# Routed experts of a mixture layer: every expert on every token, or each expert on its own tokens in 23 tiles of 128 slots

## The chip, the cores and the metric

The kernel runs on one core of a Trainium2 chip. The metric is the device time of one execution in microseconds (us); lower is better. The engines of the core work side by side: TensorE (PE, matrix products; the loading of its stationary operand is listed as PEld), VectorE (DVE), ScalarE (ACT), GpSimd (POOL) and SyncE (SP, which here only issues DMAs). Each has its own program and waits for the others on semaphores. TensorE's clock is 2.4 GHz when granted in full (shown as 1.00) and 1.2 GHz at its lower level (0.50).

## What is computed

The reference is two transformer-like layers on x of 2 x 512 tokens by 256 features: a time-mixing block, an expert-choice mixture, a delta-rule attention, and last the mixture that this change touches. Cut to that last part (D = 256, 8 experts, the two best per token, shared width 1024, routed width 128):

```
g = x @ sw1.T
u = x @ sw2.T
shared_out = jax.nn.silu(g) * u @ sw3.T
scores = jax.nn.sigmoid(x @ router_w.T)
_, top_idx = jax.lax.top_k(scores + expert_bias, TOPK)
top_scores = jnp.take_along_axis(scores, top_idx, axis=-1)
top_scores = top_scores / (top_scores.sum(-1, keepdims=True) + 1e-09)
combine = jnp.zeros((T, E), x.dtype).at[jnp.arange(T)[:, None], flat_idx].add(flat_sc)
h12 = jnp.einsum('td,ehd->teh', flat_x, w12)
h1, h2 = jnp.split(h12, 2, axis=-1)
h = jax.nn.silu(h1) * h2
out_e = jnp.einsum('teh,edh->ted', h, w3)
routed_out = jnp.einsum('ted,te->td', out_e, combine).reshape(b, s, d)
return shared_out + routed_out
```

x going in is layer-normed, and the result is layer-normed and added to x. Each of the 1024 tokens has two experts, so of the 8 x 1024 (expert, token) products that the reference writes down, 2 x 1024 have a weight other than zero.

## The kernel before

Activations lie in SBUF as 8 tiles (`NT`) of 128 tokens by 256 features. The last stage is `expert_mixture`. It turns the normed input `xm` into features-on-partitions form, splits it and all weights into a rounded part (HI, cast by ACT) and a rest (LO, a subtraction on DVE), and writes each product as three matmuls (HI*HI, HI*LO, LO*HI): `PRODUCTS`.

The work is a row of 32 steps (`STEPS`): for each half of the tokens (512), 8 blocks of 128 shared hidden features and then 8 experts of 128 hidden features, all treated alike. In a step n:

- `up(n)` (line 2108), PE: 6 matmuls for the gate and 6 for the up part, each 512 tokens wide, into a pair of PSUM banks;
- `silu(n)` (2166), ACT, on the gate; the product with the up part (2290), DVE;
- for an expert, the product with its tokens' shares (2219), POOL, which reads `share`, a 128 x 1024 tile for each expert;
- `high(n)` (2177), ACT, and the rest by POOL (2225): the two parts of the hidden features in `hidden_r`;
- `down(n)` (2124), PE, three steps (`LAG`) behind `up`: 12 matmuls of 256 columns that add to the output of the half in PSUM banks 0 to 3.

PE's order is written by hand: `up(n)`, then `down(n-3)`. Beside this, weights are cast during the first 10 steps (2146 on ACT, 2238 on DVE), two groups of four tiles a step. The router's scores come after `up(0)` (2087); DVE takes the two best (`choose`, 2252 to 2260) after step 1 and works out the shares (`weigh`, 2262) after step 2; PE turns them (2094), and SP sends them to DRAM (`share_dram`, 2196) and back, repeated on all 128 partitions (2202). At the end DVE copies the half's output from PSUM (2279), takes the statistics of the norm (292, 296), normalizes (308), adds to x (2324), and SP writes x out (2207).

## Time and profile before

| | us |
|---|---|
| median of 3 runs | 485.63 |
| lowest and highest | 484.15, 485.74 |
| the profiled execution | 489.34 |
| its span, first to last instruction | 487.6 |
| PE busy | 368.9 (76%) |
| DVE busy | 298.2 (61%) |
| ACT busy | 248.8 (51%) |
| POOL busy | 118.0 (24%) |

A chain of waits is followed back from the last instruction: at each step to what released it. PE has 29% of the span on that chain, all of it in the last stage, which starts at about 326 us. Times below count from the start of the span. "idle before" is how long an engine stood still just before an instruction, with the work that released it.

### The profile page before, as it was taken

To read this page: it belongs to the slowest core of one execution; us is meant where nothing else is said; L and a number is where in the kernel's file an instruction comes from. 1 tells how busy PE (TensorE), PEld (TensorE's weight loads), DVE (VectorE), ACT (ScalarE), POOL (GpSimd) and SP (SyncE) were. 2 spreads that over 40 slices of the span, in tenths; PEclk is the share of its full clock that TensorE was granted. 3 is DMA by queue.
4 is the path that set the end of the run, shared out by engine and by line. 5 is a ranking of instruction groups with operands and counts; after the bars stand their busy time and mean duration, and the time that the engine had idled before them with its cause. 6 is when DMAs were issued, how large, how long until landed. Compare 5 with 4: busy or idle time off the path is not lost. (4 is left out here: it accounts for less than half of the span.)

```text
span 487.6 us, 10066 instructions
## 1 busy us (share of the span) xinstructions
PE 368.9 (76%) x4130; PEld 293.4 (60%) x4130; DVE 298.2 (61%) x633; ACT 248.8 (51%) x460; POOL 118.0 (24%) x142
## 2 busy tenths in 40 slices
PE   2999877955799775332077899818999999999990
PEld 1544566855578664221066465607888888888880
DVE  5899997777245547999952667774774211311127
ACT  2889755475366755764133457547755333322230
POOL 5493002300000105000044200000244664335640
PEclk9999989888999788555579759977899999999996
DMA  7790000000000000000000000000024300000002
GB/s 230 240 342 4 0 1 0 2 0 0 1 3 2 3 3 0 1 1 0 0 1 4 3 5 3 3 1 1 0 73 146 131 0 1 1 1 2 0 1 86
DMA packets 12489, 15.82 MB, mean 32 GB/s; under 512 B 2046, under 2 KB 10644, under 8 KB 12444
## 3 DMA queue, kind: packets, MB, share of 16 engines
q1 hardware_dynamic: 12444, 15.18, 9.7%
q8 instruction: 33, 0.54, 0.5%
q14 instruction: 12, 0.10, 0.1%
HBM read 14.09 MB, written 1.08 MB: 31 GB/s over the span
## 5 line engine op out<-in xcount | busy, mean ns | idle before, releaser
L2225 POOL TENSOR_TENSOR hidden_r<-third,hidden_r 128x512 fp32r<-128x512 f32 x31 | 41.1, 1327 | 140.4 <-ACT hidden_r L2177 140.4
L2290 DVE TENSOR_TENSOR third<-third,ps 128x512 f32<-128x512 f32 x32 | 22.0, 687 | 84.8 <-PE ps L2108 79.5
L2124 PEld LDWEIGHTS ps<-down_r,hidden_r 128*128 128x128 f32 x384 | 49.2, 188 | 3.2 <-POOL hidden_r L2225 0.9
L2124 PE MATMUL ps<-down_r,hidden_r 128*128 128x256 f32 x384 | 50.3, 281 | 0.7 <-POOL hidden_r L2225 0.7
L2177 ACT CAST hidden_r<-third 128x512 fp32r<-128x512 f32 x32 | 19.9, 623 | 59.5 <-PE ps L2124 59.5
L2108 PE MATMUL ps<-xm_r,gate_r 128*128 128x512 f32 x192 | 50.1, 397 | 0.0
L2108 PE MATMUL ps<-xm_r,up_r 128*128 128x512 f32 x192 | 49.9, 396 | 0.0
L2108 PEld LDWEIGHTS ps<-xm_r,up_r 128*128 128x128 f32 x192 | 36.9, 192 | 7.9
L1509 PE MATMUL ps<-ident,area 128*128 128x128 f32 x32 | 8.5, 416 | 40.4 <-DVE area L1835 40.4
L2108 PEld LDWEIGHTS ps<-xm_r,gate_r 128*128 128x128 f32 x192 | 34.6, 191 | 5.7 <-issue 0.2
L1509 PEld LDWEIGHTS ps<-ident,area 128*128 128x128 f32 x32 | 5.6, 212 | 43.2 <-DVE area L1835 43.2
L1832 DVE TENSOR_TENSOR third<-area 128x124 f32<-128x124 f32 (+15 forms) x31 | 29.2, 943 | 1.1
L2166 ACT ACTIVATE third<-ps 128x512 f32<-128x512 f32 x32 | 19.2, 599 | 20.7 <-PE ps L2108 20.7
L1835 DVE TENSOR_TENSOR area<-area,third 128x124 f32<-128x124 f32 (+15 forms) x31 | 27.9, 901 | 1.1
L1737 ACT COPY area<-third 32x128 f32<-32x128 f32 x64 | 18.9, 295 | 14.7 <-DVE third L1879 13.4
L1681 ACT ACTIVATE area<-ps,own_side 128x512 f32<-128x512 f32 (+1 forms) x16 | 15.9, 1100 | 20.2 <-PE ps L1509 20.2
L1130 POOL TENSOR_SCALAR keys_by_head<-k_t,own_fourth 128x512 f32<-128x512 f32 x4 | 3.9, 984 | 82.8 <-ACT k_t L1275 82.8
L1162 PE MATMUL ps<-w_r,x_r 128*128 128x512 f32 x96 | 19.2, 350 | 3.6 <-DVE beta_rows L1355 2.1
L2219 POOL TENSOR_TENSOR third<-third,stored 128x512 f32<-128x512 f32 x15 | 19.4, 1291 | 0.0
L1162 PEld LDWEIGHTS ps<-w_r,x_r 128*128 128x128 f32 x96 | 14.9, 188 | 7.0 <-issue 3.5
L1180 PE MATMUL ps<-proj_rows,third 128*32 128x128 f32 x384 | 15.5, 293 | 4.7 <-ACT qkv L1301 4.0
L1582 PE MATMUL ps<-area,k_t 128*32 128x128 f32 x128 | 16.3, 353 | 1.7 <-DVE area L1888 0.7
(340 smaller groups left out, 835.1 us busy)
## 6 DMA issues: line engine op xcount, KB each, us to landing
stored<-share_dram SPq DMA_DIRECT2D x8, 512.0 KB, 5.8
stored<-in_L_ffn_sw_dram SPq DMA_DIRECT2D x3, 1024.0 KB
stored<-in_L_ffn_w_dram SPq DMA_DIRECT2D x1, 2048.0 KB
x<-L_attn_hidden_state_dram SPq DMA_DIRECT2D x4, 256.0 KB, 3.5
out_dram<-x SPq DMA_DIRECT2D x4, 256.0 KB, 2.4
w_nat<-in_L_attn_Wk_dram SPq DMA_DIRECT2D x1, 256.0 KB, 2.7
w_nat<-in_L_attn_Wv_dram SPq DMA_DIRECT2D x1, 256.0 KB, 2.9
w_nat<-in_L_attn_Wr_dram SPq DMA_DIRECT2D x1, 256.0 KB, 4.1
```

The source lines that it names most:

```text
L1162: last = nc.tensor.matmul(ps[:, bank, 0:cols.stop - cols.start], own, w_r[:, wp, ci, cols], start=i == 0, stop=i == len(passes) - 1)
L1582: last = nc.tensor.matmul(ps[strand[q], WS_BANK, 0:P], w_t[:, n, q, :], state_before(n)[:, q], start=True, stop=True, skip_group_check=True)
L1737: nc.scalar.copy(u_place[strand[q], n % U_SLOTS, :, q, :], u[strand[q], n % U_KEPT].rearrange("p (h e) -> p h e", h=HH)) \
L1832: link(V.tensor_tensor(part, rows.unsqueeze(3).to_broadcast([P, below, G, j + 1]), inv[:, j, :, 0:j + 1].unsqueeze(1).to_broadcast([P, bel ...
L1835: last = V.tensor_tensor(inv[:, j + 1:, :, 0:j + 1], inv[:, j + 1:, :, 0:j + 1], part, ALU.subtract)
L2108: last = nc.tensor.matmul(ps[:, bank + which, :], w[:, wp, c, a, :], xm_r[:, xp, c, b * T:(b + 1) * T], start=i == 0, stop=i == C * len(PR ...
L2124: last = nc.tensor.matmul(ps[:, t // 2, t % 2 * D:(t % 2 + 1) * D], hidden_r[:, n % 2, hp, t * P:(t + 1) * P], down_r[:, wp, a, :], start= ...
L2166: a(gated[:, n % 2, :], ps[:, 4 + 2 * (n % 2), :], ACT.Silu).then_inc(silu_ready, 1)
L2177: nc.scalar.copy(hidden_r[:, n % 2, HI, :], hidden[:, n % 4, :]).then_inc(hidden_hi, 1)
L2219: nc.gpsimd.tensor_tensor(hidden[:, n % 4, :], hidden[:, n % 4, :], share[:, a - SH, b * T:(b + 1) * T], ALU.mult) \
L2225: nc.gpsimd.tensor_tensor(hidden_r[:, n % 2, LO, :], hidden[:, n % 4, :], hidden_r[:, n % 2, HI, :], ALU.subtract).then_inc(hidden_lo, 1)
L2290: V.tensor_tensor(hidden[:, n % 4, :], gated[:, n % 2, :], ps[:, 4 + 2 * (n % 2) + 1, :], ALU.mult) \
```

## The change

The routed experts leave the row of steps. The steps are now 16, shared features only (`STEPS` = B * SH). After step `EARLY` = 10 come 23 tiles (`SLOTS`) of 128 token slots; each tile belongs to one expert, whose number is only known at run time. 23 = 16 full tiles for 2048 rows and at most 7 more, since an expert's last tile may be partly filled.

- After the choice of experts, PE counts (`count`, two matmuls with a table of ones and a triangle): for each token, how many before it went to the same expert. DVE makes of that a slot number for each token's first and second expert (`place_tokens`: 12 small instructions up to `slots`, 3 more up to `owner`, the expert of each tile).
- POOL writes the rows of `xm` to those slots in DRAM by 16 indirect DMAs of 128 rows of 1 KB (`rows_dram`); SP reads them back as tiles (`rows`), 8 tiles and then 15.
- For each tile j, PE turns the rows (2 transposes), loads the owner's number into a register (`own_expert`), multiplies with weights at an address made of that register (`up_routed`, 6 matmuls of 256 columns: gate and up side by side), turns the product (1 transpose) and multiplies down (`down_routed`, 3 matmuls of 256 columns). ACT makes the rounded parts, the silu, and copies the result out (`keep_rows`); DVE makes the rests and the product.
- SP writes the results to DRAM in four parts, POOL gathers them again by 16 indirect DMAs (`found`), and DVE adds them with the shares (`combine`).
- POOL no longer computes in the stage; the rest of `hidden_r` is made by DVE. The shares are no longer turned, nor sent through DRAM.
- Early in the program three DMAs fill `rows_dram` with input rows, so that unused slots hold finite numbers, and 16 more small memsets run on POOL.

```diff
+    SLOTS = 2 * NT + E - 1
+    STEPS, EARLY, LAG = B * SH, 10, 3
+    SLOTS_FIRST = NT
+    RESULT_PARTS = ((0, 8), (8, 16), (16, 20), (20, SLOTS))
...
+                def own_expert(j):
+                    expert[j] = nc.tensor.value_load(owner[0:1, j:j + 1], min_val=0, max_val=E - 1)
...
+                def turn_rows(j):
+                    if j in (0, SLOTS_FIRST):
+                        pe.wait_ge(rows_in[j // SLOTS_FIRST], 16)
...
+                def up_routed(j):
+                    pe.wait_ge(xm_lo_kept, TURNED + j + 1)
+                    pe.wait_ge(prod_ready, tile(j - 2) if j >= 2 else shared(EARLY - 2 + j))
+                    if j == 0:
+                        pe.wait_ge(kept_dve, len(groups))
+                    for i, (c, wp, xp) in enumerate((c, *parts) for c in range(C) for parts in PRODUCTS):
+                        last = nc.tensor.matmul(ps[:, 4 + j % 2, 0:2 * P], rows_t[j % 2][:, xp, c],
+                                                routed_up[:, wp, c, bass.DynSlice(expert[j], 1), :], start=i == 0,
+                                                stop=i == C * len(PRODUCTS) - 1)
...
+                for j in range(SLOTS + 2):
+                    if j < SLOTS:
+                        turn_rows(j)
+                        own_expert(j)
+                    if j < LAG:
+                        down(EARLY - LAG + j)
+                    if 1 <= j <= SLOTS:
+                        up_routed(j - 1)
+                    if j >= 3:
+                        turn_hidden(j - 3)
+                    if j >= 4:
+                        down_routed(j - 4)
+                up(EARLY)
+                turn_hidden(SLOTS - 1)
+                down_routed(SLOTS - 2)
+                down_routed(SLOTS - 1)
+                for n in range(EARLY + 1, STEPS + LAG):
                     if n < STEPS:
                         up(n)
...
+                sp.wait_ge(rows_out, 16 * 2 * NT)
...
+                for start, stop in RESULT_PARTS:
+                    sp.wait_ge(rows_kept, stop)
+                    sp.dma_start(tiles(core.results_dram)[:, start:stop, :], rows[:, start:stop]) \
+                        .then_inc(results_out, 16)
...
+                pool.wait_ge(routed, PLACED)
+                for t in range(NT):
+                    for k in range(2):
+                        nc.gpsimd.indirect_dma_start(core.rows_dram, bass.IndirectOffsetOnAxis(slots[:, k, t:t + 1], 0),
+                                                     xm[:, t, :], None).then_inc(rows_out, 16)
+                pool.wait_ge(results_out, 16 * (1 + len(RESULT_PARTS)))
+                for t in range(NT):
+                    for k in range(2):
+                        nc.gpsimd.indirect_dma_start(found[:, k, t, :], None, core.results_dram,
+                                                     bass.IndirectOffsetOnAxis(slots[:, k, t:t + 1], 0)) \
+                            .then_inc(results_in, 16)
...
+                def keep_first():
+                    dve.wait_ge(down_done, SH)
+                    dve.wait_ge(rows_out, 16 * 2 * NT)
                     for t in range(TB):
...
+                def combine(t):
+
+                    if t < TB:
+                        link(V.scalar_tensor_tensor(y[:, t], found[:, 0, t], share[:, 0, t:t + 1], y[:, t], ALU.mult,
+                                                    ALU.add))
+                    else:
+                        link(V.tensor_scalar(y[:, t], found[:, 0, t], share[:, 0, t:t + 1], None, ALU.mult))
+                    return V.scalar_tensor_tensor(y[:, t], found[:, 1, t], share[:, 1, t:t + 1], y[:, t], ALU.mult,
+                                                  ALU.add)
...
+                dve.wait_ge(results_in, 16 * 2 * NT)
+                for t in range(NT):
+                    last = combine(t)
```

PE's program before, in the middle of the row of steps: one `up` and one `down`, and so on to the end of the stage (names after "waits" are semaphores).

```order
713 L2108 MATMUL ps<-xm_r,gate_r 128x512 [waits prod_ready,xm_lo_kept,ffn_w_kept_dve]
714 L2108 MATMUL ps<-xm_r,gate_r 128x512 x5
715 L2108 MATMUL ps<-xm_r,up_r 128x512 x6
716 L2124 MATMUL ps<-down_r,hidden_r 128x256 [waits ffn_w_kept_dve,hidden_lo]
717 L2124 MATMUL ps<-down_r,hidden_r 128x256 x11
```

```order
831 L2202 MATMUL ps<-ident,stored 128x128 [waits xm_lo_kept]
832 L2202 MATMUL ps<-ident,stored 128x128
833 L2192 TENSOR_LOAD owner
834 L2192 ISA x2
835 L2212 ISA [waits prod_ready,xm_lo_kept]
836 L2212 MATMUL ps<-routed_up,xm_r 128x256 x2
837 L2212 ISA
838 L2212 MATMUL ps<-routed_up,xm_r 128x256
...
843 L2221 MATMUL ps<-ident,stored 128x128 [waits hidden_lo,prod_ready]
844 L2228 REGISTER_ALU [waits routed_rows_kept,hidden_lo]
845 L2228 MATMUL ps<-routed_down,xm_r 128x256 x2
```

Where one step had 24 matmuls of two widths and no register, one tile has 12 matmuls and transposes with a register load and some address arithmetic between them.

POOL's program in this stage before (its first rows; the pair L2219, L2225 goes on in this way):

```order
68 L2225 TENSOR_TENSOR hidden_r<-third,hidden_r 128x512 [waits hidden_hi] x2
69 L2225 TENSOR_TENSOR hidden_r<-third,hidden_r 128x512 [waits down_done,hidden_hi] x6
70 L2219 TENSOR_TENSOR third<-third,stored 128x512 [waits prod_ready,share_in_first]
71 L2225 TENSOR_TENSOR hidden_r<-third,hidden_r 128x512 [waits down_done,hidden_hi]
72 L2219 TENSOR_TENSOR third<-third,stored 128x512 [waits prod_ready,share_in_first]
```

POOL's program in this stage after:

```order
68 L2366 MEMSET third 128x128
69 L2367 AFFINE_SELECT third<-third 128x128 [waits masks_order]
70 L2374 DMA rows_dram<-xm,slots 2944x256 [waits tokens_routed,f_in,masks_order]
71 L2374 DMA rows_dram<-xm,slots 2944x256 x15
72 L2379 DMA stored<-results_dram,slots 128x256 [waits rows_in_second]
73 L2379 DMA stored<-results_dram,slots 128x256 x15
```

47 computing instructions have gone, and 32 indirect DMAs have come, in two runs of 16, each behind one wait.

## Rows read from the trace of the kernel before

**Rows 1.** The chain of waits, in order of time: start, us, what.

```profile
351.67 1.41 PE ps L2124 x12
...
353.08 2.73 PE ps L2108 x12
```

**Rows 2.** Who waited for whom in 335 to 490 us: total, times, longest.

```profile
POOL hidden_r L2225 <- ACT hidden_r L2177: 140.4, 31, 74.7
DVE third L2290 <- PE ps L2108: 79.5, 27, 3.5
```

**Rows 3.** Stretches: length, busy by engine, granted clock, DMA share, GB/s.

```profile
352.00:378.00 26.00, 26.00 (x156) 22.70 (x155) 16.10 (x31) 13.49 (x24) 10.16 (x7) 1.00 0.33 104
...
433.00:470.00 37.00, 37.00 (x217) 32.75 (x217) 6.69 (x10) 10.83 (x18) 20.25 (x16) 1.00 0.00 1
```

**Rows 4.** Timeline of PE: start, us, engine, line, operation, count, idle before.

```profile
72.03 2.78 PE L129 MATMUL ps<-ident,stored 128*128 128x128 f32 x24
...
255.95 0.75 PE L1543 MATMUL ps<-area,n_t 64*32 64x64 f32 x52 [1.11 <-issue]
...
341.63 2.16 PE L2108 MATMUL ps<-xm_r,gate_r 128*128 128x512 f32 x6
343.58 2.63 PE L2108 MATMUL ps<-xm_r,up_r 128*128 128x512 f32 x6
...
377.35 1.57 PE L2124 MATMUL ps<-down_r,hidden_r 128*128 128x256 f32 x12
```

**Rows 5.** Stretches with transposes alone on PE: columns as in Rows 3.

```profile
72.03:74.81 2.78, 2.78 (x25) 2.54 (x23) 2.68 (x10) 2.15 (x5) 0.00 (x0) 1.00 0.02 6
...
245.10:250.40 5.30, 5.30 (x27) 5.30 (x26) 2.83 (x7) 2.09 (x2) 0.00 (x0) 0.50 0.00 0
```

**Rows 6.** Timeline of DVE around the choice of experts.

```profile
346.32 0.69 DVE L2290 TENSOR_TENSOR third<-third,ps 128x512 f32<-128x512 f32 x1 [2.45 <-PE ps L2108]
...
350.91 0.16 DVE L2259 FIND_INDEX8 where<-best,select 128x8 uint32<-128x8 f32 x1
...
353.53 0.23 DVE L2267 TENSOR_TENSOR first<-first,second 128x64 f32<-128x64 f32 x1
353.79 0.23 DVE L2268 TENSOR_TENSOR first<-first,scores 128x64 f32<-128x64 f32 x1
```

**Rows 7.** Timeline of POOL: the same instruction twice.

```profile
359.02 2.57 POOL L2225 TENSOR_TENSOR hidden_r<-third,hidden_r 128x512 fp32r<-128x512 f32 x1 [3.85 <-ACT hidden_r L2177]
363.15 1.29 POOL L2225 TENSOR_TENSOR hidden_r<-third,hidden_r 128x512 fp32r<-128x512 f32 x1 [1.57 <-ACT hidden_r L2177]
```

**Rows 8.** Timeline of SP's queue: issuing one DMA.

```profile
7.98 0.47 SPq L166 DMA_DIRECT2D third<-in_L_ffn_expert_b_dram  x1
```

**Rows 9.** DMA issues: KB each, median us from issue to landing.

```profile
out_dram<-x SPq DMA_DIRECT2D x4, 256.0 KB, 2.4
```

**Rows 10.** A stretch of DMA traffic: POOL busy, granted clock, DMA share, GB/s.

```profile
360.00:370.00 10.00, 4.17 (x3) 1.00 0.63 215
```

**Rows 11.** Groups by form: count, busy us, mean ns, idle before.

```profile
L1719 ACT COPY k_t<-ps 128x256 f32<-128x256 f32 x4 | 1.5, 378 | 0.0
...
L907 ACT ACTIVATE raised<-logits 128x128 f32<-128x128 f32 x1 | 0.3, 309 | 2.9 <-DVE logits L949 2.9
...
L1019 DVE TENSOR_TENSOR x<-x,xf 128x256 f32<-128x256 f32 x8 | 3.3, 410 | 0.6 <-ACT xf L272 0.6
L998 DVE SCALAR_TENSOR_TENSOR over<-left,least 128x256 f32<-128x256 f32 x1 | 0.5, 483 | 0.0
```

**Rows 12.** Timeline of the end of the kernel.

```profile
475.27 1.42 DVE L2279 COPY xm<-ps 128x256 f32<-128x256 f32 x4 [2.43 <-PE ps L2124]
476.73 1.41 DVE L292 BATCH_NORM_STATS2 ln_stats<-xm 128x6 f32<-128x256 f32 x4
```

398 lines of the change are left out of this document (267 added, 131 removed).

## The prediction

> **What bounds the kernel now.** I read the chain of waits first. In the last stage it is PE alone: `down`, 1.41 us, then `up`, 2.73 us, in turn to the end [rows 1]. The stretches agree: PE is busy all of the time from 352 to 378 and from 433 to 470 us, at the full 2.4 GHz, while DVE is busy 16.1 of 26 us, later 6.7 of 37 [rows 3]. The list of waits says the same from the other side: POOL waited 140.4 us for ACT, DVE 79.5 us for PE [rows 2]. So here time is what PE has to do, 32 steps of 4.14 us = 132.5 us, and the tail behind it. A cut in PE's work counts in full, until something else is late. What the change puts beside PE are transfers and register loads of which this trace has none; they decide.
>
> **What PE loses and gains.** A `down` matmul of 256 columns takes 1.41 / 12 = 0.118 us [rows 1], a transpose 2.78 / 24 = 0.116 us at the full clock [rows 4]. 16 steps go: -66.2 us. 23 tiles come, each with 9 matmuls of 256 columns and 3 transposes: 1.06 + 0.35 = 1.41 us, together +32.4 us. If nothing else changed, 34 us would be won. The rest of the working is what of this is given back, as a line of times on the profiled execution.
>
> **Where the slots are known.** The product of step 1 starts at 346.3 us [rows 6]. Behind it now stand one rest (0.6) and one weight group (0.6) instead of two groups, then the choice. In the trace that starts at 348.96 and its last instruction ends at 351.1 [rows 6]: 2.1 us. Then three small instructions, 0.8 us. PE's `count` can so start at about 351.5, when `up(3)` is done; it takes some 0.5 us. DVE comes to `place_tokens` after the product and the rest of step 3, and that rest waits for `down(0)`: about 355.5 us. There are 12 instructions in a chain up to `slots`; the like of them stand 0.26 us apart (353.53 to 353.79) [rows 6], so 3.3 us with the longer scan: POOL gets its slots at 358.8 us. PE doesn't wait for this; DVE gets fuller in steps 4 to 9 (product, rest, up to three groups, and `weigh`: about 3.5 of PE's 4.14 us a step), close, but below PE.
>
> **The scatter.** 16 indirect DMAs on POOL, one after the other. The trace has no DMA issued by POOL. Below, SP's 0.47 us for an issue [rows 8]; above, POOL's 1.29 us for a full-width instruction, and 2.57 us for the same one when DVE works on two tiles in SBUF at the same time [rows 7]. I take 1.0 us, nearer to POOL's row, since POOL makes 128 addresses by software, though with less data than 128 x 512. 16 x 1.0 = 16.0, so 374.8; 2.4 us to land, as a store of 256 KB [rows 9]: 377.2. Then SP reads 1 MB back: 4.9 us at the 215 GB/s of [rows 10], and 1.5 us for the way: the first tile can be turned at 383.6 us. PE, with `down(6)`, is ready at about 378.4 (it ends at 378.9 in the trace [rows 4], with the turning of shares in front of it, which goes). PE stands still for 5.2 us. The three `down`s left over would fill 4.2 us of it, but `turn_rows(0)` stands ahead of them. After the pause the clock may be low: the twelve matmuls from 341.63 took 4.4 us where 2.73 is usual [rows 4]. I add 1.5 us.
>
> The Trainium skill (GPSIMD Engine Reference, section Key points) says that GpSimd shares its SBUF interfaces with VectorE and contends with DVE instructions that have two SBUF inputs. The doubled row agrees, 2.57 for 1.29 us. The scatter runs just when DVE is full of such subtractions, the gather when it is less so.
>
> **The 23 tiles.** PE needs 1.41 us a tile. ACT has two copies of 256 columns and two instructions of 128, 2 x 0.378 + 2 x 0.309 = 1.37 us; DVE 0.41 and two shorter ones, about 1.0 us [rows 11]. So ACT is just behind PE. Unknown is the register: one load, two checks and six small pieces of address work a tile in PE's sequencer. Below: nothing, if the sequencer runs ahead and PE has matmuls queued, 1.41 us. Above: the longest pause of PE for which the profile names no releaser, 1.11 us [rows 4], each time: 2.52 us. I take 1.8, since there is some queue, but the load stands right behind only two transposes. 23 x 1.8 = 41.4 us. Beside them are three `down`s (4.2 us), the wait of `down(8)` for DVE's four copies in `keep_first` (1.2 us, 1.42 less a transpose pair; it is 1.42 in [rows 12]), and at the end `up(10)` and the last tile's passage through ACT and DVE (2.7 + 1.7 us). The last result is in SBUF at 383.6 + 1.5 + 41.4 + 4.2 + 1.2 + 4.4 = 436.3 us.
>
> The Trainium skill (DMA: Bandwidth & Descriptors, section Latency and other measured facts) gives a floor of about 600 ns for a `tensor_load`. Laid on PE bare, the tile would be 2.0 us and the sum 4.8 us longer; no run here shows it yet.
>
> **The way back.** The last part of the results, 3 tiles, goes out in 3.4 us, 16 gathers take 16.0 at the same price, 2.4 to land: 458.1 us. PE meanwhile has 5 `up`s and 6 `down`s, 22.1 us, and about 1 us more since `high(n)` waits for `down(n-2)`: 459.4 us. The two are level; but behind the gather stands work on DVE that was not there. `combine` is 16 instructions of 0.41 to 0.48 us [rows 11], 7.2 us, then four tiles' statistics, 1.4 us, which stood beside PE before: 466.7. Then four additions, 1.6 us: 468.3 us. From there on it is as before from 476.73 to 487.6 [rows 12]: 10.9 us. Sum: 479.2 us against 487.6, so -8.4 us. The profiled execution has 1.7 us around its span and is 3.7 us above the median; I take the difference over to the median: 485.63 - 8.4 = 477.2 us.
>
> The terms that can move are in one line: span = 405.8 + 32 x (POOL's price of an indirect DMA) + 23 x (price of a tile), as long as POOL is later than PE at both ends. With 1.0 and 1.8 that is 479.2.
>
> **Costed at nothing.** The 16 memsets stand in front of a wait of POOL for a DMA, early in the kernel. The three filling DMAs run after the last weight load, where the transfers are idle. The rests that DVE takes over from POOL are 0.69 us and have over 3 us of DVE's waiting in each late step [rows 2]. If that cover went, each would cost 0.6 us.
>
> **Rivals.** *Both unknowns are cheap.* POOL at 0.47, tile at 1.41: the rows are there before PE is (375.1 < 378.4), the last result at 378.4 + 32.4 + 4.2 + 1.2 + 4.4 = 420.6, PE ends at 443.7, and the span is 456.1: 454 us. For it: SP issues as fast as that. Against it: POOL is the slow one wherever both do the same work.
>
> *The register load stalls PE each time.* Tile at 2.5 us: 16 us more, 495 us of span, 493. For it: the load is an instruction of the sequencer and what follows needs it. Against it: PE runs queued work while its sequencer is busy, and turning, `down` and `up` of other tiles lie between the load and its use.
>
> *POOL is slow: the case on the other side.* Its place is the two runs of 16, its price 32 times the excess. With the tile at 1.8 it eats the gain from 1.26 us on, just about the 1.29 of an ordinary full-width instruction [rows 7]; at 2.0 us the span is 511, 509 us. For it: the doubled row. Against it: a DMA of 128 rows asks less of POOL than 512 columns on 128 partitions.
>
> *The clock.* Transposes alone ran 2.78 us at 1.00, but 5.3 us at 0.50 after a pause [rows 5]. If PE stays at 1.2 GHz through the tiles, one costs 2 x 1.41 = 2.8 us: 23 us more, 500 us. The Trainium skill (TensorE: Matmul & The Clock Gate, section Part 4: PE-mode transpose) says that transposes do not engage the full clock. Against this rival: three of four instructions here are matmuls, and wide ones.
>
> **How the numbers follow.** Forecast and its neighbourhood (POOL 0.8 to 1.3, tile 1.5 to 2.2): 0.45; both cheap: 0.15; the load stalls: 0.17; POOL slow: 0.15; clock: 0.08. A measurement of this kernel can tell about 0.3% (1.5 us) from no change. Faster is the second case, 0.38 of the first and 0.03 of the third: 0.56; same 0.06; slower 0.38. The range leaves out the lower part of the cheap case and the upper part of the slow ones: 458 to 502. Faster and slower both have weight; the forecast's own range is 467 to 490 us.
>
> **What would show it.** Right: 16 POOL issues about 1.0 us apart from 359 us; PE still from 378 to 384 us; tiles 1.8 us apart; the gather landing within 2 us of PE's last `down`; 21 us from there to the end, with DVE's 16 additions ahead of the old tail. Wrong: issues over 1.26 us apart, tiles over 2.2 us apart, or a clock of 0.50 between 390 and 430 us. Wrong the other way: tiles at 1.4 us and no pause of PE before the first.

## The result, and the profile after

The changed kernel takes 495.03 us (median of 4 executions, 493.87 to 495.45) beside 485.69 us for the kernel before in the same session. The ratio is 1.020, 95% interval 1.017 to 1.023: 2.0% slower. The forecast was 477.2 us, 1.7% faster. Its range (458 to 502) holds the result, its sign was wrong. Executions of one kernel can lie 2% apart (the kernel before took 484.15 to 495.25 us here), and the profiled executions of gather_late, changed_again and all_three_paused below are such longer ones, so the experiments compare stages rather than whole executions.

The page of the changed kernel, busy time of each engine, and the stretches of its last stage (length, then busy us of PE, PEld, DVE, ACT and POOL, granted clock, DMA share, GB/s):

```profile
PE 345.4 (70%) x4018; PEld 271.0 (55%) x4018; DVE 325.6 (66%) x735; ACT 253.9 (51%) x520; POOL 91.0 (18%) x146
```

```profile
345.00:380.00 35.00, 30.14 (x173) 25.98 (x171) 23.95 (x79) 14.53 (x27) 17.22 (x16) 1.00 0.17 61
380.00:392.00 12.00, 4.59 (x21) 3.87 (x22) 7.08 (x14) 3.65 (x8) 0.00 (x0) 0.72 0.76 251
392.00:420.00 28.00, 25.96 (x184) 23.20 (x184) 12.28 (x40) 13.84 (x51) 0.00 (x0) 0.94 0.11 39
420.00:440.00 20.00, 17.83 (x120) 14.98 (x118) 8.32 (x29) 10.88 (x39) 0.00 (x0) 1.00 0.23 80
440.00:470.00 30.00, 22.24 (x107) 18.40 (x108) 6.09 (x11) 6.19 (x12) 15.18 (x16) 0.90 0.27 84
```

PE's work did shrink: 345.4 us instead of 368.9. But between 380 and 392 us, where PE was busy without a gap before (below), it is now busy for 4.6 us of 12, and it is slow again after 458 us.

```profile
380.00:392.00 12.00, 12.00 (x72) 10.65 (x71) 2.06 (x3) 3.61 (x6) 7.32 (x6) 1.00 0.16 63
```

What stands ahead of the last stage is the same code in both kernels but for the filling DMAs and the memsets, yet its length varies: the first `up` starts at 334.9 us in the profile of before and at 332.0 in that of after, and between 330 and 341 us in the profiles of the experiments. So below I compare profiled executions by the **last stage**, from the start of `up(0)` to the end: 487.6 - 334.9 = 152.7 us before, 493.1 - 332.0 = 161.1 us after, 8.4 us more. The prediction's line of times gives 479.2 - 334.9 = 144.3 us. The 16.8 us between forecast and measurement lie here (us from the start of `up(0)`, or lengths):

| piece | predicted | measured |
|---|---|---|
| slots known, scatter starts | 23.9 | 24.1 |
| from there to the first tile's turning | 24.8 | 28.6 |
| from there to the last result in SBUF | 52.7 | 56.8 |
| from there to the last gathered row | 21.8 | 24.1 |
| from there to the end | 21.1 | 27.6 |

Timelines of POOL: the first scatter issues, the last, then the first gather issues. Start, duration, and in brackets how long POOL stood idle before:

```profile
356.05 1.20 POOL L2374 DMA_INDIRECT rows_dram<-xm,slots  x1 [32.01 <-DVE owner L2446]
357.56 1.43 POOL L2374 DMA_INDIRECT rows_dram<-xm,slots  x1 [0.30 <-issue]
...
367.83 0.96 POOL L2374 DMA_INDIRECT rows_dram<-xm,slots  x1 [0.30 <-issue]
...
376.88 0.96 POOL L2374 DMA_INDIRECT rows_dram<-xm,slots  x1 [0.30 <-issue]
```

```profile
444.20 0.98 POOL L2379 DMA_INDIRECT stored<-results_dram,slots  x1 [66.36 <-DMA results_dram<-stored]
445.48 0.96 POOL L2379 DMA_INDIRECT stored<-results_dram,slots  x1 [0.30 <-issue]
```

An indirect DMA of 128 rows keeps POOL busy for 0.95 us and 0.30 us pass to the next: 1.25 us each. In the scatter four of the first five take 1.20 to 1.48 us. The scatter lasts 356.05 to 377.84, 21.8 us, the gather 19.75 us, where 16.0 each was predicted. Below them PE, the start of the tiles:

```profile
384.62 0.69 PE L2202 MATMUL ps<-ident,stored 128*128 128x128 f32 x2 [7.12 <-DMA stored<-rows_dram]
385.60 2.90 PE L2182 MATMUL ps<-down_r,hidden_r 128*128 128x256 f32 x12 [0.29 <-issue]
388.30 0.61 PE L2202 MATMUL ps<-ident,stored 128*128 128x128 f32 x2
```

`down(7)` takes 2.90 us after the pause, twice the 1.41 of [rows 1]. Then the tiles, the first matmul group of two in a row:

```profile
411.41 0.97 PE L2212 MATMUL ps<-routed_up,xm_r 128*128 x6 [0.18 <-DVE stored L2479]
...
413.16 0.98 PE L2212 MATMUL ps<-routed_up,xm_r 128*128 x6
```

Seventeen steps from 400.68 to 432.38 give 1.865 us a tile. The last surprise is behind them. PE by its own records, then ACT's `high(n)`, which waits for `down(n-2)`:

```profile
453.95 1.58 PE L2182 MATMUL ps<-down_r,hidden_r 128*128 128x256 f32 x12
455.37 1.55 PE L2166 MATMUL ps<-xm_r,gate_r 128*128 128x512 f32 x6
...
462.57 0.38 PE L2182 MATMUL ps<-down_r,hidden_r 128*128 128x256 f32 x1 [1.03 <-issue]
463.98 0.57 PE L2182 MATMUL ps<-down_r,hidden_r 128*128 128x256 f32 x1 [1.03 <-issue]
```

```profile
452.73 0.62 ACT L2294 CAST hidden_r<-third 128x512 fp32r<-128x512 f32 x1 [6.22 <-PE ps L2182]
...
466.90 0.62 ACT L2294 CAST hidden_r<-third 128x512 fp32r<-128x512 f32 x1 [13.05 <-remote]
```

By its matmul records `down(11)` (the twelve from 453.95 us) is over at 455.5, but the `high(13)` that waits for it starts at 466.90. PE itself then issues single matmuls 1.4 us apart, waiting for nothing that the profile shows. The trace also has marks of the moments at which semaphores were raised. Some are missing, in the scatter above all (the ups' semaphore has 52 marks for 55 steps); from the gather's start on those of PE's ups (each up has two) and downs are complete:

```
ups    443.2 444.5 445.9 447.2 448.6 450.0 456.2 461.1 466.9 467.0
downs  452.7 466.8 467.1 471.2 473.8 475.4
```

Up to 450.0 they come as the work is done. Then hardly one comes in 5 us, and at 466.8 to 467.1 four come in a burst: `down(11)`, both of `up(15)`, `down(12)`. The last packet of the gather is at 465.3 us, its last landing mark at 465.5. I call these PE's **held signals**. Between the first and the last of the four lie 4.2 us of matmuls (an `up` and a `down`), so the work of `down(11)` was done at least 4 us before its mark, and 11 us before by PE's own records: it is the signal that is late.

### The profile page after: what moved, and what is told of

It is laid out like the page before. It is cut to its first block and busy times, and to the rows that moved or that the text cites. A ratio compares the mean times of both kernels' runs of the same rounds, so it can differ in the third digit from the quotient of the medians.

```text
span 493.1 us, 10184 instructions
## 1 busy us (share of the span) xinstructions
PE 345.4 (70%) x4018; PEld 271.0 (55%) x4018; DVE 325.6 (66%) x735; ACT 253.9 (51%) x520; POOL 91.0 (18%) x146
## 5 line engine op out<-in xcount | busy, mean ns | idle before, releaser
L2182 PE MATMUL ps<-down_r,hidden_r 128*128 128x256 f32 x192 | 31.8, 320 | 9.6 <-issue 5.9
L2182 PEld LDWEIGHTS ps<-down_r,hidden_r 128*128 128x128 f32 x192 | 29.4, 225 | 12.3 <-issue 9.7
L2294 ACT CAST hidden_r<-third 128x512 fp32r<-128x512 f32 x16 | 9.9, 620 | 38.1 <-remote 18.6
L1520 PEld LDWEIGHTS ps<-ident,area 128*128 128x128 f32 x32 | 5.1, 194 | 43.4 <-DVE area L1846 43.4
L2379 POOL DMA_INDIRECT stored<-results_dram,slots x16 | 15.2, 949 | 70.9 <-DMA results_dram<-stored 66.4
L2166 PE MATMUL ps<-xm_r,gate_r 128*128 128x512 f32 x96 | 26.1, 408 | 2.6 <-DVE up_r L2393 2.1
L2212 PE MATMUL ps<-routed_up,xm_r 128*128 x138 | 22.8, 302 | 3.6 <-DVE stored L2479 2.9
L2166 PE MATMUL ps<-xm_r,up_r 128*128 128x512 f32 x96 | 24.4, 389 | 0.0
L2374 POOL DMA_INDIRECT rows_dram<-xm,slots x16 | 17.2, 1076 | 36.6 <-DVE owner L2446 32.0
L2212 PEld LDWEIGHTS ps<-routed_up,xm_r 128*128 128x128 f32 x138 | 18.5, 195 | 8.0 <-issue 8.0
L2166 PEld LDWEIGHTS ps<-xm_r,gate_r 128*128 128x128 f32 x96 | 17.9, 197 | 6.5 <-DVE up_r L2393 2.3
L2462 DVE TENSOR_TENSOR third<-third,ps 128x512 f32<-128x512 f32 x16 | 10.9, 683 | 15.5 <-PE ps L2139 6.0
L2166 PEld LDWEIGHTS ps<-xm_r,up_r 128*128 128x128 f32 x96 | 18.0, 188 | 3.8
```

Source lines behind the costliest of these rows:

```text
L2166: last = nc.tensor.matmul(ps[:, bank + which, :], w[:, wp, c, a, :], xm_r[:, xp, c, b * T:(b + 1) * T], start=i == 0, stop=i == C * len(PR ...
L2182: last = nc.tensor.matmul(ps[:, t // 2, t % 2 * D:(t % 2 + 1) * D], hidden_r[:, n % 2, hp, t * P:(t + 1) * P], down_r[:, wp, a, :], start= ...
L2212: last = nc.tensor.matmul(ps[:, 4 + j % 2, 0:2 * P], rows_t[j % 2][:, xp, c], routed_up[:, wp, c, bass.DynSlice(expert[j], 1), :], start=i ...
L2294: nc.scalar.copy(hidden_r[:, n % 2, HI, :], hidden[:, n % 4, :]).then_inc(hidden_hi, 1)
L2374: nc.gpsimd.indirect_dma_start(core.rows_dram, bass.IndirectOffsetOnAxis(slots[:, k, t:t + 1], 0), xm[:, t, :], None).then_inc(rows_out, 16)
L2379: nc.gpsimd.indirect_dma_start(found[:, k, t, :], None, core.results_dram, bass.IndirectOffsetOnAxis(slots[:, k, t:t + 1], 0)) \
```

## The experiments

Each ran beside the kernel before on the same chip. Ratios are to it. "First tile" is the first routed matmul, "gather" the start of the gather or of what stands in its place, both from `up(0)`; "to end" runs from the gather to the end.

| kernel | median us | ratio [95%] | last stage | first tile | gather | to end |
|---|---|---|---|---|---|---|
| changed | 495.03 | 1.020 [1.017, 1.023] | 161.1 | 61.4 | 112.2 | 48.9 |
| gather_late | 512.39 | 1.053 [1.046, 1.061] | 177.0 | 63.0 | 134.8 | 42.2 |
| pe_padded | 496.32 | 1.022 [1.012, 1.031] | 158.5 | 59.8 | 109.7 | 48.8 |
| downs_first | 499.11 | 1.028 [1.016, 1.039] | 159.6 | 61.3 | 110.7 | 48.9 |
| fixed_weights | 487.86 | 1.005 [1.001, 1.009] | 152.0 | 60.8 | 103.2 | 48.8 |
| plain_gather_pool | 486.72 | 0.999 [0.994, 1.004] | 154.2 | 63.5 | 114.9 | 39.3 |
| plain_gather_sp | 486.83 | 0.997 [0.992, 1.002] | 150.6 | 61.3 | 111.0 | 39.6 |
| registers_spread | 489.96 | 1.007 [1.003, 1.011] | 156.7 | 65.9 | 107.8 | 48.9 |
| half_rows | 476.62 | 0.980 [0.974, 0.986] | 142.5 | 53.3 | 103.2 | 39.3 |
| gather_later | 499.03 | 1.027 [1.019, 1.034] | 163.8 | 62.2 | 119.2 | 44.6 |
| changed_again | 497.49 | 1.018 [1.011, 1.025] | 162.8 | 62.5 | 114.0 | 48.8 |
| two_pauses | 493.68 | 1.014 [1.008, 1.019] | 157.1 | 61.9 | 113.3 | 43.8 |
| tail_early | 489.89 | 1.008 [1.004, 1.012] | 155.4 | 62.2 | 112.4 | 43.0 |
| all_three_spread | 485.12 | (two groups, below) | 142.6 | 58.7 | 99.2 | 43.3 |
| all_three_paused | 485.23 | 0.987 [0.983, 0.992], its five lower executions of 12 | 154.0 | 69.6 | 110.4 | 43.6 |
| all_three_again | 481.72 | 0.988 [0.983, 0.992] | 143.1 | 59.1 | 99.8 | 43.3 |
| all_four | 472.98 | 0.972 [0.967, 0.978] | 139.6 | 59.2 | 99.7 | 39.9 |

The last four columns come from one profiled execution of each kernel.

### Does PE crawl by itself, or beside the gather?

```diff
+                pool.wait_ge(down_done, shared(STEPS - 1))
                 for t in range(NT):
                     for k in range(2):
                         nc.gpsimd.indirect_dma_start(found[:, k, t, :], None, core.results_dram,
```

> One wait is added to the changed kernel: GpSimd starts its 16 gathers only after PE's last down. Nothing of the computation is left out. In the changed kernel PE crawls from 458.7 to 467 us, one matmul each 1.4 us, while the gather runs (444 to 466 us). Theory A, the gather's transfers hold up PE's supply of instructions: without a gather beside it PE runs down(11) and the rest at 0.118 us a matmul and ends its last down at about 467 us; the gather then takes 16 x 1.25 + 2.4 = 22.4 us, the tail 20: span about 509.5 us, time 511.5. Theory B, PE crawls at this place of its program whatever runs beside: last down at 475.4, span about 517.8, time 520.

Last stage 177.0 us. PE's timeline after the tiles, without a gather beside it:

```profile
465.88 1.55 PE L2166 MATMUL ps<-xm_r,gate_r 128*128 128x512 f32 x6
467.26 1.52 PE L2166 MATMUL ps<-xm_r,up_r 128*128 128x512 f32 x6
468.62 4.72 PE L2182 MATMUL ps<-down_r,hidden_r 128*128 128x256 f32 x36
```

`down(12)` to `down(14)`, which took from 458.1 to 473.8 us in the changed kernel, run through in 4.7 us. Theory A: 161.1 plus the expected 16.4 (a span of 509.5 less 493.1) is 177.5. The crawl needs the gather.

### The pause before the tiles, and the place in PE's program

```diff
+                pe.wait_ge(routed, OWNED)
+                for i in range(48):
+                    nc.tensor.matmul(ps[:, 2, 0:D], down_r[:, HI, 0, 0:P], down_r[:, HI, 1, :], start=True, stop=True)
                 for j in range(SLOTS + 2):
```

> The changed kernel with 48 more matmuls of 256 columns, whose results nobody reads, between down(6) and turn_rows(0): 48 x 0.118 = 5.7 of PE's 7.1 us idle time before the first tile. Theory A, the pause costs clock: with the pause filled, down(7) to down(9) take 1.41 us each instead of 2.90, 2.23 and 1.9, so the tiles begin about 2.8 us earlier. Rival: the wait for keep_first and for ACT and DVE takes it back, under 1 us. On the crawl of PE during the gather: if it belongs to a fetch of PE's instructions, it moves with the program, 96 instructions (some 5 to 6 us of ups and downs) earlier, to about 450 us, or falls apart; if it belongs to the gather alone, it stays at 14 us after the gather's start. Time 492 if A holds and the crawl stays as long, 484 if the crawl goes.

```profile
386.32 1.63 PE L2182 MATMUL ps<-down_r,hidden_r 128*128 128x256 f32 x12 [0.59 <-issue]
...
390.86 1.62 PE L2182 MATMUL ps<-down_r,hidden_r 128*128 128x256 f32 x12 [2.69 <-DVE xm L2494]
```

With the pause filled, the granted clock stays at 2.4 GHz (1.00 from 380 to 392 us, where the changed kernel had 0.72), `down(7)` to `down(9)` take 1.6 to 1.7 us, and the gather starts 2.5 us earlier: the clock's part of the late start, as expected. The run times do not show it: 1.022 beside 1.020, where 492 us was expected. The crawl was to move if it belonged to a fetch of PE's instructions, and did not:

```profile
460.50 0.37 PE L2182 MATMUL ps<-down_r,hidden_r 128*128 128x256 f32 x1 [1.03 <-issue]
```

It begins 15 us after the gather's start as before (14.5). The trace's queue of instruction packets (q8, 16 KB at a time) agrees: one is sent 11.7 us after the gather's start in the changed kernel and 2.7 us after it here, with the crawl at the same distance in both.

### The downs first

```diff
+                for j in range(LAG):
+                    down(EARLY - LAG + j)
                 for j in range(SLOTS + 2):
                     if j < SLOTS:
                         turn_rows(j)
                         own_expert(j)
-                    if j < LAG:
-                        down(EARLY - LAG + j)
```

> The changed kernel with down(7), down(8) and down(9) of PE ahead of turn_rows(0), and what belongs to them on ACT (the copy of hidden rows) and DVE (the rest, keep_first) ahead of the first tile's copies. All of the computation is there. Theory A: the pause of 7.1 us before the first tile takes up the downs and the wait for keep_first, 2.90 + 2.50 + 2.23 + 1.9 = 9.5 us go from behind the read, of which perhaps 1.5 come back as slow clock in the first tiles: last result about 8 us earlier, 433 us, and with the crawl of PE unchanged in length a time of about 487 us. Rival: keep_first waits for the scatter to land (379.5 us) and down(8), down(9) follow at half clock up to 388 us, behind the read: a gain of 4 us or less.

```profile
380.40 2.35 PE L2182 MATMUL ps<-down_r,hidden_r 128*128 128x256 f32 x12 [3.62 <-DVE hidden_r L2466]
386.03 5.46 PE L2182 MATMUL ps<-down_r,hidden_r 128*128 128x256 f32 x24 [3.29 <-DVE xm L2490]
```

1.5 us gained in the last stage, not 8: the rival. In the run times there is no gain: the four executions took 492.8 to 505.2 us, and 487 was expected. `down(7)` waited 3.6 us for a rest of DVE, which stood behind ACT's `high(7)` at 379.0: the signal of `down(5)`, recorded as over at 372.6, came at 378.9. So PE's signals are held at the end of the scatter too; in the changed kernel that of `down(5)` came at 379.6, which cost it little, since the rows landed at 384.6. Then `keep_first`, which must wait for the scatter, and two downs near half the clock: 2.73 us each, with 0.54 granted from 384 to 392 us.

### What the register costs

```diff
-                    expert[j] = nc.tensor.value_load(owner[0:1, j:j + 1], min_val=0, max_val=E - 1)
+                    expert[j] = j % E
```

> The changed kernel without the register: each tile takes the weights of expert j mod 8 at a fixed address, so routed results are of other experts than the tokens chose; all else is there. Theory A, the register's load and the address work set the tile's price: without them a tile goes from 1.87 us to what PE and ACT need, 1.41 to 1.45 us, 23 x 0.43 = 10 us less, time about 485 us. Rival, the tile is set by the chain of semaphores from PE over ACT and DVE and back: it stays at 1.8 to 1.87 us, time 494 to 495.

The chain of waits of this kernel, one tile and the start of the next:

```profile
405.50 0.72 PE ps L2212 x6
406.21 0.11 PE ps L2221
406.32 0.36 PE ps L2228 x3
406.68 0.22 PE ps L2202 x2
406.90 0.71 PE ps L2212 x6
```

From one tile to the next it is 1.40 us (406.90 - 405.50), all of it PE's matmuls. So the register is 0.47 us of a tile's 1.87, and 9.1 us of the last stage. Is it the load, or the address work that stays when the loads are moved?

```diff
+                            if FIRST_LOAD <= n < EARLY and i % 2 and len(expert) < SLOTS:
+                                own_expert(len(expert))
                             last = nc.tensor.matmul(ps[:, bank + which, :], w[:, wp, c, a, :],
```

> The changed kernel with the 23 register loads moved from the tiles into up(6) to up(9), one ahead of every other matmul; all of the computation is there. Theory A, the load (0.31 to 0.55 us in PE's sequencer, and 0.15 us of bounds) is what a tile pays and the address pieces in front of the matmuls cost next to nothing: a tile takes 1.40 to 1.50 us as with fixed weights, 23 x 0.4 = 9 us less, time about 486 us, and PE has slack in those four ups (rows land at 384.6 us), so up to 4 us of slowing there are free. Rival, the address pieces are a good part of the price: a tile of 1.6 to 1.7 us, time 489 to 491 us. The gather keeps 1.25 us an issue and PE's late signals stay.

A tile takes 1.40 to 1.41 us again, so the address pieces cost nothing that can be seen, and the load with its bounds all of the 0.47. In the sequencer's records of the changed kernel 18 of the 23 loads last 0.30 to 0.31 us and five 0.49 to 0.92, with 0.15 for the bounds. My reading, which no run tests, is that it isn't hidden because PE has only few matmuls queued ahead of it. But the last stage shrank by 4.4 us only. The first tile came 4.5 us later than in the changed kernel: in this execution `down(6)` crawled, from 372 us on, beside the scatter, and PE was back at its pace at about 381 us:

```profile
375.02 0.28 PE L2186 MATMUL ps<-down_r,hidden_r 128*128 128x256 f32 x1 [1.03 <-issue]
```

### Which DMAs hold PE's signals?

```diff
-                        nc.gpsimd.indirect_dma_start(found[:, k, t, :], None, core.results_dram,
-                                                     bass.IndirectOffsetOnAxis(slots[:, k, t:t + 1], 0)) \
+                        nc.gpsimd.dma_start(found[:, k, t, :], tiles(core.results_dram)[:, 2 * t + k, :]) \
```

> The same with the 16 plain DMAs issued by GpSimd in the place of the 16 indirect ones (rows in order, not by index, so the combined rows are not the tokens' own). If DMAs that GpSimd makes hold up PE's signals whatever their kind, down(11) signals at the end of the stream again, 9 us or more late; if it takes the lists of indices, PE keeps its 4.2 us a step and its last down ends at about 467 us. For the issue price: 1.25 us as for the indirect ones if a GpSimd DMA costs the same whatever the index, under 1 us if the index is what costs.

"The same" is plain_gather_sp, where SP issues the 16 plain DMAs.

POOL's groups, then ACT's `high(12)` and `high(13)`:

```profile
L2379 POOL DMA_DIRECT2D stored<-results_dram x16 | 8.6, 574 | 68.2 <-DMA results_dram<-stored 68.2
```

```profile
452.45 0.62 ACT L2294 CAST hidden_r<-third 128x512 fp32r<-128x512 f32 x1 [4.95 <-PE ps L2182]
456.61 0.62 ACT L2294 CAST hidden_r<-third 128x512 fp32r<-128x512 f32 x1 [3.04 <-PE ps L2182]
```

`high(n)` comes each 4.16 us, and PE's last down ends 20.6 us after the gather's start instead of 31.2. As many bytes to the same places, issued by POOL, hold nothing when no list of indices is used; and they cost 0.54 us each instead of 1.25. The same 16 plain DMAs issued by SP gave a last down at 467.0 us and a last stage of 150.6 us, without held signals too. So plain DMAs held none. They were also over sooner: their last packet came 10.4 us after the first issue, beside 21.1 us for the indirect ones. No run has a stream of plain DMAs as long as that; the nearest pair is this one and the 8 indirect DMAs of half_rows, below, which took 11.2 us and did hold one signal. The kernel is level with the one before (0.999), by the held signals gone and by the cheaper row; two_pauses, below, parts the two.

### How many of them, and when?

```diff
-                    for k in range(2):
+                    for k in range(1):
                         nc.gpsimd.indirect_dma_start(core.rows_dram, bass.IndirectOffsetOnAxis(slots[:, k, t:t + 1], 0),
```

> The changed kernel with 8 instead of 16 indirect DMAs in the scatter and in the gather: only each token's first expert is served, the second one's rows are left out. Theory A, the price of an indirect DMA is 1.25 us each in a row: the scatter ends 10 us earlier, its landing is at about 369, so rows are there before PE has done down(6) at 377.5, the pause of PE goes; the gather of 8 ends 10 us earlier, at about 437 + 12.5. PE's late signals: in the gather they began 6 us and more after its start; if that needs a long row of them, 8 DMAs (10 us) hold up at most one signal, for 3 to 5 us, and PE's last down ends at about 461 to 463 us. Span about 477 to 479 us. Theory B, any indirect DMA holds the signals till all have landed: the first signal held is the one nearest to the gather's middle, and the burst comes at the last packet, 13 us after the gather's start.

The last stage is 18.6 us shorter. The gather of 8 held one signal for 3 us: the ups' marks are 439.3, then 444.8 and 444.9 for the two that were due at 442.1 and 443.4, when the last packet had landed. Behind the burst all is regular. The last down ended at 454.1 us and the span was 472.8, both earlier than expected (461 to 463, 477 to 479). The scatter held none that anyone waited for, and PE had no pause but that for `keep_first`.

```diff
+                pool.wait_ge(up_done, ups(EARLY + 3))
                 for t in range(NT):
```

> The changed kernel with one more wait: GpSimd's gather starts only when up(13) has been signalled, at about 450 instead of 444.2 us. Nothing is left out. Theory A, the held signals belong to the time since the gather's start (one signal late by about 1 us after 6 us, then hardly one in 5 us until the last packet): down(10) and down(11) signal on time at 451.4 and 455.6 us, the next ones are held until about 472 us, PE's last down ends near 476 us or before. Rival, they belong to a place in PE's program: down(11) is again the one that is held, from 455 us on.

The gather started at 449.2. `down(10)` and `down(11)` signalled on time, 449.8 and 454.0; then 466.2, and a burst at 471.9 and 472.1; the gather's last packet is at 470.4. The hold began one step later in PE's program: theory A. The last down ended at 476.3 us, as expected.

```diff
                 for t in range(NT):
+                    if t == NT // 2:
+                        pool.wait_ge(results_in, 16 * NT)
                     for k in range(2):
                         nc.gpsimd.indirect_dma_start(found[:, k, t, :], None, core.results_dram,
```

(and the same ahead of the ninth scatter, on `rows_out`)

> The changed kernel with one wait in each row of 16 indirect DMAs: GpSimd issues 8, waits till they have landed, and issues the other 8. Nothing is left out. Each pause costs 2.9 us less the 0.3 of an issue, 2.6 us: rows and gather each later by that, +5.2 us in sum on the path from the slots to the gathered rows. Theory A, the held signals of PE cost the last 9 us and need a row longer than some 6 to 10 us (8 DMAs held one signal for 3 us): PE's last down comes 22 to 24 us after the gather's start instead of 31, the gather ends 22.9 + 2.6 us after its start and then sets the end: from the gather's start to the span's end 25.5 + 20 = 45.5 us instead of 48.9. With 2.6 us lost before the first tile: last stage 160.5 us, about the same as the changed kernel. Rival, the signals are held in short rows just as long: last stage 166 us or more.

> The changed kernel itself, nothing altered, beside the variants on one chip. By the profiled executions so far, what comes before the last stage varies from run to run (its first up starts between 330 and 341 us), and the last stage itself is steady: 161.1 us from the first up to the end, 152.7 in the kernel before. Expected here: 161 to 163 us again, a ratio of 1.015 to 1.025 to before.

POOL at the pause, and ACT's `high(13)` and `high(14)`:

```profile
457.35 0.94 POOL L2383 DMA_INDIRECT stored<-results_dram,slots  x1 [0.30 <-issue]
460.36 0.94 POOL L2383 DMA_INDIRECT stored<-results_dram,slots  x1 [2.07 <-DMA stored<-results_dram,slots]
```

```profile
460.14 0.62 ACT L2294 CAST hidden_r<-third 128x512 fp32r<-128x512 f32 x1 [1.95 <-PE ps L2182]
464.15 0.62 ACT L2294 CAST hidden_r<-third 128x512 fp32r<-128x512 f32 x1 [2.89 <-PE ps L2182]
```

Three of PE's marks come at 459.9 to 460.1, in the moment the first eight have landed; the next are regular. PE's last matmul ends 20.6 us after the gather's start, as with plain DMAs. From the gather to the end it is 43.8 us instead of 48.8 and 48.9, 5 us less though the gather itself takes 1.8 us more. In the scatter the pause cost nothing that can be seen (first tile at 61.9 us; 61.4 and 62.5 without). The last stage, 157.1, is better than the 160.5 expected. By the run times alone two_pauses and changed_again can't be told apart: 1.014 [1.008, 1.019] and 1.018 [1.011, 1.025].

### The exposed combine

> The changed kernel with combine alone rearranged: four semaphores instead of one for the gathered rows, three of the four pairs of token tiles combined in DVE's pause ahead of low(13), statistics right behind. Nothing is left out. DVE is idle from 454.7 to 467.5 us, while three pairs are there by 462; behind PE's last down remain the fourth pair (1.7 us, beside PE's last two downs), the four additions and the old tail: last stage 161.1 - 6.5 = 154.6 us, a ratio of 1.003 to 1.01 to before. Rival: reading the gathered tiles beside GpSimd's issues makes both slower, the gain is under 3 us.

```diff
                 for n in range(EARLY + 1, STEPS):
                     product(n)
+                    if n == COMBINE_STEP:
+                        for i in range(3):
+                            combine_pair(i)
                     low(n)
```

(`COMBINE_STEP` is 13; `combine_pair(i)` waits for the four gathers of two token tiles, combines these and takes their statistics.) It took 5.7 us off the last stage: DVE did 12 of the 16 additions from 456.3 to 464.2 while it had nothing else, and behind PE's last down the end came 12.4 us later instead of 17.7.

### Together

The edits of downs_first, registers_spread and tail_early in one kernel:

> The changed kernel with three edits, nothing left out: the three downs ahead of the first tile, the register loads in up(6) to up(9), and the 16 additions of combine in pairs of token tiles with a semaphore of their own, three pairs in DVE's pause before the rest of step 13. On the profiled executions so far: 491.0 us with the downs first, 9 us less for the registers, and of the 6.8 + 1.4 us of combine and statistics 5.1 + 1.4 go under the gather: 491 - 9 - 6.5 = 475.5 us of span, time 477, some 1.7% faster than before. If PE's late signals end with the last packet of the gather as they did, PE's last down is the bound and not the gather. Rival: DVE, waiting for gathered rows in the order of its program, holds low(13) and so PE beyond the end of the gather: 480 us or more.

Its six executions were 474.7, 477.6 and four at 484.9 to 486.3 us, two groups some 9 us apart. The profiled one, of the lower group, had a last stage of 142.6 us. So I ran it again, with its own forecast:

> The same kernel as all_three_spread, nothing left out, timed once more, since its executions fell into two groups, 475 to 478 and 485 to 486 us. If the second group has PE's signals held in the scatter too (as the profiled execution of registers_spread, where down(6) took from 372 to 381 us, and as that of all_three_spread had not), the same two groups come again, 10 us apart, whatever the kernel before does beside them; if it was the chip, there is one group near 475 to 478 us.

Six executions on another chip: four from 478.1 to 481.8, two at 487.9 and 491.3, beside 482.9 to 490.7 for the kernel before; the ratio is of the four. Two groups again, less clearly apart.

```diff
                 for t in range(NT):
+                    if t and t % 2 == 0:
+                        pool.wait_ge(results_in[t // 2 - 1], 16 * 4)
                     for k in range(2):
```

> The kernel with the three edits (downs first, registers in the ups, combine in pairs) and one more: GpSimd's gather waits after each 4 of its 16 indirect DMAs until they have landed, so it takes three pauses of 2.9 us and 3.8 us less issue each, some 8 us more in all. Nothing is left out. Theory A, PE's held signals are let out whenever no indirect DMA is under way: PE's last down comes at 452 to 455 instead of 460.5 us, the gather ends at 460 instead of 451.5 us, and both together give about the same span as without pauses, 472 to 474 us. Rival, the signals are held by each indirect DMA in its own time: PE's last down moves little and the span is 3 us or more longer.

Half right. Up to `up(15)` PE's marks came on time (450.6, 452.0, 454.8, 456.1), and from the gather to the end it took 43.6 us beside 43.4 without the pauses. But PE's last down did not come earlier: `low(13)` stands behind the third pair of `combine` in DVE's program, and that pair landed later. The first tile started at 69.6 us instead of 58.7: in this execution PE crawled from 370 to 379 us beside the scatter, and the last stage took 154.0 us. That fits the upper group, but it isn't shown to be its cause: only one execution of a kernel is profiled, and what stands ahead of the last stage varies by as much.

Last the three edits with the two pauses of two_pauses:

> The kernel with three edits (downs first, registers in the ups, combine in pairs) and the two pauses after 8 indirect DMAs. Nothing is left out. Without the pauses its last stage took 142.6 and 143.1 us, and 154.0 when PE's signals were held in the scatter too. Theory A: the pauses cost 2.6 us ahead of the first tile, nothing behind (the gather had 10 us of slack behind PE's held downs, and PE's downs end 5 us earlier or more), and no execution has the scatter's signals held for 10 us: last stage 141 to 145 us in all executions, one group of times near 475 to 478 us plus what the stages before vary. Rival: held signals in the scatter come from something else than the length of the row, and the second group, 8 to 10 us higher, is there again.

Six executions from 471.6 to 477.4 us, one group; ratio 0.972 [0.967, 0.978], 2.8% faster than before and 4.5% faster than the changed kernel of that session by their ratios (0.9723 / 1.0182). The three edits without the pauses had 0.988 [0.983, 0.992] on another chip. The pauses behind the first 8 gathers and the first 8 scatters came together, and six executions can't tell whether the pause in the scatter or chance kept the upper group away. The chain of waits at its end:

```profile
436.03 1.41 PE ps L2186 x12
437.44 2.75 PE ps L2170 x12
...
445.76 5.79 issue
451.56 6.21 PE ps L2186 x36
457.86 1.43 DVE xm L2555 x4
```

All of the computation is there. What is left is the 5.79 us in front of the last three downs, again `low(13)` behind the third pair.

## Why the prediction was wrong, point by point

- **What bounds the kernel before, PE's share.** Right in kind: the tiles' own matmuls are 1.40 us, as computed (1.41). PE's busy time fell by 23.5 us (368.9 to 345.4), not by the 33.8 of the sum: with the register loads the six `up` matmuls of a tile are spread over 0.98 us instead of 0.71, and the downs behind both pauses ran below the full clock.
- **The slots at 358.8 us.** Right: 23.9 us after `up(0)` predicted, 24.1 measured.
- **POOL's price, 1.0 us.** Wrong, and the first of the two steps that turned the sign. The price was set at 1.0 us; it was chosen "nearer to POOL's row" of 1.29 [rows 7] and should have stayed at it: 1.25 in the gather, 1.36 on average in the scatter. The 0.30 us between two issues was no term at all. 21.8 + 19.75 - 32 = 9.5 us too little. The text's own break-even was 1.26 us; the mean is 1.30. The rival "POOL is slow" happened at that price, and half_rows speaks for it: with 16 of the 32 left out, 18.6 us went, the held signals among them.
- **Contention of POOL and DVE.** The Trainium skill (GPSIMD Engine Reference, section Key points) says that GpSimd contends with DVE instructions of two SBUF inputs. The trace agrees in part: 1.20 to 1.48 us for four of the first five scatters, three of them beside such subtractions, and 0.95 in the gather; but the scatters at 366.57 and 367.83 took 0.96 us beside such subtractions too.
- **The ways between.** Landing and reading back took 6.8 us after POOL's last scatter, not 8.8. The last results went out in 2.8 us, not 3.4, and the last gather landed in 1.5, not 2.4. Together these are 3.5 us less.
- **The tile, 1.8 us.** Right in sum, 1.87, and in its reason: fixed_weights and registers_spread give 0.47 us to the register load. "PE has matmuls queued" was the half that does not hold. The Trainium skill (DMA: Bandwidth & Descriptors, section Latency and other measured facts) has a floor of 600 ns for a `tensor_load`; 18 of the 23 loads here are below it, at 0.30 to 0.31 us.
- **The start of the tiles.** 1.5 us for the clock was too small: `down(7)` to `down(9)` took 7.0 instead of 4.2 us (2.8 us more), and pe_padded got 2.5 us back. The wait for `keep_first` was 2.50 instead of 1.2 us, and 2.69 at the full clock in pe_padded: `high(9)` (0.62) and its rest (0.69) stand ahead of it in the program, which the sum left out.
- **PE at the end, 459.4 us, "level" with the gather.** Wrong, the second step: 475.4. Nothing in the trace of before could show it, since it has no indirect DMA. The line "as long as POOL is later than PE at both ends" was the condition that broke. The forecast had PE and the gather level and no wait between them; measured, PE's held signals put its last `down` 9.9 us behind the last landing (465.5), and DVE's combine, which stands behind the rests of the last steps, starts at 472.6. In the line of times it is 6.5 us; two_pauses took back 5.
- **The tail.** Right: 16 additions, statistics, four additions, old tail, 20.5 us from the first addition to the end, 21.1 predicted from the last row.
- **Costed at nothing.** The memsets, filling DMAs and DVE's rests stayed hidden; `up(4)` waited 2.09 us for DVE's weights, which PE's later pause made up for.
- **The clock through the tiles.** This rival did not happen: 0.94 was granted from 392 to 420 us and 1.00 from 420 to 440.

The parts add up: 9.5 us for POOL's price less 3.5 for shorter ways, 4.1 for the tiles and their start, 6.5 for the held signals and 0.2 for the slots are the 16.8 us.

What stays open: by what way an indirect DMA holds back signals of PE, whether a plain stream of 20 us would do so too, and why the hold in the scatter costs the first tile nothing in most profiled executions, but 4.5 us in registers_spread and 10.9 in all_three_paused. The Trainium skill (SBUF — State Buffer, section SBUF: two separate sides) says that compute engines and DMAs cannot slow each other there. The runs do not speak against that for the data; what comes late here is the signal. A hint lies in the marks: the 16 plain gathers of plain_gather_pool left 256 landing marks, 16 each, and the 16 indirect ones of the changed kernel 66. In two_pauses the first 8 left 48, and still POOL's wait for all 128 ended at the last of them (460.1 us). So marks are missing or stand for several steps at once, and the signals of the DMAs themselves look different too; the runs don't say more.

## What to carry to other kernels

Price a row of indirect DMAs by POOL at 1.25 us for each 128 rows and the landing, and ask first whether that row fits beside other work; here POOL was busy or between issues for 41.5 us with 32 of them, more than the 33.8 us of PE work that was to be saved. Load registers for a loop of short tiles ahead of it, under wide matmuls. And when indirect DMAs run beside a pipeline that passes signals back and forth, break them into groups that land (8 here), and let every consumer take what has landed instead of waiting for all.

## What the hardware showed unexpectedly

- While 16 indirect DMAs run, PE's semaphores come late from some 6 to 9 us after their start: one in 5 us, the rest in a burst (four within 0.3 us) 1.3 us after the last landing. PE then issues single matmuls 1.4 us apart. Groups of 8 held a signal for 3 to 4 us; 16 plain DMAs from POOL or SP, over in about 10 us, held none.
- The records of PE's matmuls do not show this: `down(11)` stands there 11 us before its signal. The engine that waits (here ACT, 13.05 us, with "remote" as releaser) and the marks of the semaphores do.
- A plain DMA of 128 rows costs POOL 0.54 us, one with a list of indices 1.25 us.
- Nearly the same code ahead of the last stage took 330 to 341 us from one profiled execution to another; comparing from `up(0)` on took this out.
